# Reordering queues and the row chain of a fused ConvNeXt block and window graph block, and splitting its MLP step over halves and quarters of TensorE's array

## The chip, the cores and the metric

The kernel runs on one core of a Trainium2 chip. The metric is device time in microseconds (us) of one execution; three executions of the kernel before are the base. Lower is better.

## What is computed

The input `x` is 32 images of 24 channels, 56 by 56 pixels, in float32. Two blocks follow each other:

```python
# block 1 (ConvNeXt)
h = depthwise_conv_7x7(x) + conv_b
h = (h - mean_c(h)) * rsqrt(var_c(h) + 1e-5) * ln_g + ln_b     # over the 24 channels of a pixel
h = gelu(h @ w1 + b1)                                          # 24 -> 96
x1 = (h @ w2 + b2) * layer_scale + x                           # 96 -> 24
# block 2 (window graph)
y = (fc1(x1)) * s1 + t1                                        # 1x1 convolution
nodes = windows of 8 x 8 pixels of y                           # 64 nodes of 24 channels
idx = the 9 nearest nodes of each node, by distance of the normalised channel vectors
h = max over the 9 of gelu(([x_i, x_j - x_i] @ ew.T + eb) * es + et)   # 48 channels
out = fc2(h) * s2 + t2 + x1                                    # 48 -> 24
```

## The kernel before, in words

The program writes its own instruction streams for five engines (TensorE, VectorE, ScalarE, GpSimd and the DMA queue on SyncE), tied by semaphores. There is no scheduler: the order in each stream is the order in the code, and every engine works its stream in order. It has three stages.

**Convolution** (to about 200 us). Lines 861 to 876 on TensorE; the change does not touch it.

**MLP stage** (about 203 to 553 us), 56 steps `m` (`NSTEP`). A step takes four groups of 24 channels (32 partitions each, 24 of them used) by `L` = 448 pixels. Its parts on TensorE are functions: `centre` (L888, subtract the channel mean by a matmul, into bank 0), `variance` (L897, four matmuls with the squares of 112 pixels each as weights and 4 columns), `turn_std` (L904, four transposes of the spread reciprocal deviations, into bank 1), `expand` (L914, 24 to 96 channels: three matmuls of 128 by 128 by 448) and `contract` (L920, back to 24, four matmuls of 128 by 64 by 448 in column halves). `mlp_slot` (L930) orders them: contract of step m-1, centre of m+3, expand of m, turn of m+1, variance of m+3. VectorE's own `mlp_slot` (L712) does `residual(m-1)`, `spread_std(m+2)`, `normalise(m+1)`, `add_eps(m+3)`. GpSimd does one power per step (`inv_std`, L347), ScalarE one square, one copy and three gelus. `turn_std(m+1)` may overwrite bank 1 only after `normalise(m)` has read it (`at_least(pe, hn_d, m)`). SyncE loads `ht` (convolution output, `load_h`), `xt` (the input, `load_x`) and stores `x1_d` (`store_x1`) per pair of steps, four DMAs each.

**Graph stage** (about 581 to 2187 us). 28 iterations `i` (`NI`, strips of 8 image rows), each of 7 windows `wx`; one window is a "slot", 196 in all. In a slot `pe_slot` (L1068) finds distances for the window three ahead (`dist`), ranks for the one two ahead (`transpose`, `ranks`, `project`), splits projections into three bfloat16 parts (`subtract`), and gathers the neighbours by one-hot matmuls (`gather`, 3 of 12 matmuls each). VectorE (`dve_slot`, L802) reduces what was gathered (6 `reduce`, L783), builds eight one-hot masks (`make_onehot`, L770), takes the top 8 (L756) and marks them (L762). GpSimd's `pool_slot` (L389) adds the query term (`add_q`, L369).

Once per iteration, between the slots, stand the parts of the "row chain" for the next iteration: `fc1` in slots 5 and 6, `make_y` on ScalarE (L467), `norm` (L962, slot 0), the power on GpSimd (`inv_norm`, L361), `spread_norm` on VectorE (L747), `turn_norm` (L968, slots 1 and 2), `take_norm` on ScalarE, `scale_y` on GpSimd (L377, slot 2), `square_xa`, `halfsq` (L977, slot 3), `take_xb` (L488), four `spread_xa` copies on ScalarE (L494, slots 2 and 3: the four 32-partition blocks of `xa` go to a block-diagonal tile `xam`), six `node_terms` (L1004, placed by the table `QS_AT`) and `fc2` of the iteration before (L995, slots 4 and 5). `dist` waits for `xb_done` and `xam_done`. `node_terms` reads `y2`, which SyncE copies from `yb` (`load_y2`, L281, 12 DMAs), queued behind `store_iter`, `load_res` and `load_iter`.

The loops over pairs of iterations turn back at slot 0 of an even iteration on TensorE, and at slot 0 of an odd one on VectorE, ScalarE and GpSimd.

## Time and profile before

| | us |
|---|---|
| median of 3 runs | 2190.81 |
| lowest and highest | 2185.35, 2200.28 |
| the profiled execution, its own time | 2189.12 |
| its span, first to last instruction | 2187.2 |

Busy over the span: TensorE matmul 1919.6 us (88%), its weight loads 899.0 (41%, beside the matmuls), VectorE 1521.0 (70%), ScalarE 1113.3 (51%), GpSimd 643.8 (29%). The mean granted TensorE clock is 0.94 of full. The table shows what engines did, not what they cost: an idle engine costs nothing unless the chain that sets the end runs through it. Ends of matmuls are modelled, so distances between starts say more than durations; these are used below.

### The profile page before, as it was taken

The page shows a single profiled execution, that of the slowest core. Times are in us where ns is not written, and L with a number is a line of the kernel's source. Part 1 is how long each engine was busy: PE and PEld are TensorE (multiplying, and loading weights), DVE is VectorE, ACT ScalarE, POOL GpSimd, SP SyncE. Part 2 cuts the span into 40 slices and gives each one's busy share as a digit, 9 for nine tenths or more (in the row PEclk, how much of TensorE's full clock was granted, in tenths as well). Part 3 has the DMA queues.
Part 4 walks back from the last instruction along what each step waited for, and adds up shares of the span by engine and source line. Part 5 has one row for each costly group of instructions (what it writes and reads, how often), then busy time and mean ns, then how long its engine had stood idle before and what let it go on. Part 6 is the DMA issues. An engine that isn't in the chain of part 4 may idle for free.

```text
span 2187.2 us, 49786 instructions
## 1 busy us (share of the span) xinstructions
PE 1919.6 (88%) x16042; PEld 899.0 (41%) x16042; DVE 1521.0 (70%) x5840; ACT 1113.3 (51%) x2630; POOL 643.8 (29%) x407
## 2 busy tenths in 40 slices
PE   6998999999788898898888888888888888889886
PEld 2444555555333343343433333434343433434332
DVE  4222222222398889788888888888888888888897
ACT  0012444444465556565555555555555555656563
POOL 3002444444122322222222232222222222223232
PEclk9997999999799989899999999999999899989999
DMA  7872333333201111110111111111111111111010
GB/s 142 148 147 68 83 85 83 85 81 80 57 14 33 33 34 29 29 27 21 29 33 34 33 33 33 34 33 33 33 33 33 34 33 31 28 25 28 23 38 14
DMA packets 161305, 105.54 MB, mean 48 GB/s; under 512 B 120640, under 2 KB 158272, under 8 KB 160960
## 3 DMA queue, kind: packets, MB, share of 16 engines
q1 hardware_dynamic: 161088, 102.63, 20.5%
q8 instruction: 138, 2.26, 0.4%
q14 instruction: 79, 0.65, 0.1%
HBM read 54.40 MB, written 28.90 MB: 38 GB/s over the span
## 4 chain that ended last, share of the span: by engine, by line
PE 45%; issue 25%; ACT 12%; DVE 9%; POOL 6%; SPq 1%; DMA 1%; POOLq 0%; DVEq 0%; ACTq 0%
PE bank L867 7%; PE bank L1063 6%; PE bank L918 6%; PE bank L995 5%; ACT xam L494 4%; DVE red L783 4%; PE bank L926 4%; PE bank L892 3%; POOL hq L369 3%; POOL rn L361 2%; PE bank L1034 2%; ACT pb L510 2%; PE bank L1018 2%; PE bank L901 2%; DVE onehot L770 2%
## 5 line engine op out<-in xcount | busy, mean ns | idle before, releaser
L783 DVE TENSOR_REDUCE red<-bank 128x64 f32<-128x512 f32 x1176 | 751.6, 679 | 221.1 <-PE bank L1063 202.7
L510 ACT CAST pb<-bank 64x192 bf16<-64x192 f32 x1176 | 367.6, 313 | 391.7 <-PE bank L1034 361.5
L1063 PE MATMUL bank<-onehot,pb 128*32 128x512 bf16 x7056 | 517.3, 401 | 4.6 <-DVE red L783 4.0
L369 POOL TENSOR_TENSOR hq<-red,arena 128x384 f32<-128x384 f32 x196 | 201.8, 1029 | 548.5 <-DVE red L783 537.8
L350 POOL TENSOR_TENSOR rs<-ve,mhalf 112x16 f32<-112x16 f32 x56 | 162.4, 2899 | 351.6 <-DVE ve L689 351.6
L770 DVE TENSOR_SCALAR onehot<-slot 128x256 bf16<-128x256 bf16 x1568 | 244.2, 227 | 0.0
L1004 PE MATMUL bank<-arena,wqs 128*128 128x448 f32 x336 | 174.9, 605 | 55.3 <-DMA arena<-yb 51.6
L1063 PEld LDWEIGHTS bank<-onehot,pb 128*32 128x32 bf16 x7056 | 137.3, 97 | 183.4 <-issue 84.6
L361 POOL TENSOR_TENSOR rn<-nv,mhalf 128x28 f32<-128x28 f32 x28 | 135.9, 4854 | 219.3 <-DVE nv L742 219.3
L867 PE MATMUL bank<-arena,toep 120*120 120x448 f32 x384 | 161.6, 582 | 21.4 <-DVE arena L621 21.4
L1034 PE MATMUL bank<-pb,nidentb 128*128 128x192 bf16 x784 | 139.0, 261 | 38.8 <-ACT pb L510 38.8
L762 DVE MATCH_REPLACE8 marked<-t,bank 128x64 bf16<-128x64 f32 x784 | 158.2, 211 | 0.0
L1012 PE MATMUL bank<-negb,identb 128*128 128x256 bf16 x196 | 56.7, 289 | 113.1 <-DVE marked L762 50.4
L1018 PE MATMUL bank<-xb,xam 128*64 128x64 f32 x3136 | 143.2, 238 | 0.0
L756 DVE MAX8 t<-bank 128x8 f32<-128x64 f32 x784 | 119.8, 211 | 32.4 <-PE bank L1018 32.4
L918 PE MATMUL bank<-hn,w1g 128*128 128x448 f32 x336 | 137.3, 545 | 0.0
L377 POOL TENSOR_TENSOR xa<-rnt,yb 128x512 f32<-128x512 f32 (+1 forms) x56 | 63.5, 1134 | 235.4 <-ACT rnt L483 235.4
L1018 PEld LDWEIGHTS bank<-xb,xam 128*64 128x64 f32 x3136 | 115.1, 146 | 30.0 <-issue 11.3
L442 ACT ACTIVATE sq<-bank 128x448 f32<-128x448 f32 x56 | 30.4, 543 | 189.3 <-PE bank L892 189.3
L995 PE MATMUL bank<-og,f 128*128 128x448 f32 x280 | 117.4, 551 | 4.7 <-DVE og L798 4.7
L386 POOL TENSOR_TENSOR x1o<-x1o,xt 128x448 f32<-128x448 f32 x56 | 63.9, 1142 | 184.3 <-DVE onehot L770 177.1
L867 PEld LDWEIGHTS bank<-arena,toep 120*120 120x120 f32 x384 | 70.7, 184 | 111.5 <-issue 90.1
(92 smaller groups left out, 2570.0 us busy)
## 6 DMA issues: line engine op xcount, KB each, us to landing
arena<-yb SPq DMA_DIRECT2D x336, 56.0 KB, 2.0
arena<-in_x SPq DMA_DIRECT2D x24, 392.0 KB
ht<-conv_d SPq DMA_DIRECT2D x112, 84.0 KB
xt<-in_x SPq DMA_DIRECT2D x112, 84.0 KB
x_d<-x1o SPq DMA_DIRECT2D x112, 84.0 KB
ht<-x_d SPq DMA_DIRECT2D x112, 84.0 KB
xt<-x_d SPq DMA_DIRECT2D x56, 168.0 KB, 3.2
out<-x1o SPq DMA_DIRECT2D x112, 84.0 KB, 2.0
```

The costliest lines, as they stand in the source:

```text
L361: nc.gpsimd.tensor_tensor(rn[:, :], nv[:, :], mhalf[:, :], ALU.pow).then_inc(s["rn_done"], 1)
L369: nc.gpsimd.tensor_tensor(hq[:, :, :, :], red[:, k, :, :, :], qs[:, b, :, wx, :].unsqueeze(1).broadcast_to([128, 2, T, NN]), ALU.add).then ...
L510: last = nc.scalar.copy(pb[64 * u:64 * u + 64, k, part, :, :, u, :], src[64 * u:64 * u + 64, :, :, :])
L770: last = nc.vector.tensor_scalar(onehot[:, k, :, t, :], slot[:, k, :, :], float(t + 1 - 99), None, ALU.is_equal)
L783: nc.vector.tensor_reduce(red[:, k, h, t, :], src, axis=mybir.AxisListType.X, op=op).then_inc(s["red_done"], 1)
L867: last = mm(bank[0:KC, 2 * b + ch, 0:CL].rearrange("p (b v) -> p b v", v=W2), toep[b][:, sh, :], xrow[b][:, ICH * ch:ICH * (ch + 1), 2 * s ...
L918: mm(bank[:, 3 + t, 0:L], w1g[:, t, :], hn[:, r % 2, :], start=True, stop=True).then_inc(mm1_d, 1)
L995: last = mm(bank[:, 6 + gp, 0:L], f2[:, 2 * gp + t, :], og[:, b, t, :, :, :].rearrange("p r w c -> p (r w c)"), start=t == 0, stop=t == 1 ...
L1004: mm(bank[:, 5, 0:L], wqs[:, e // T, e % T, :], y2[:, b, e % T, :, :].rearrange("p w i -> p (w i)"), start=True, stop=True).then_inc(s["qs ...
L1018: last = mm(bank[64 * h:64 * h + 64, 2, t * NN:(t + 1) * NN], xam[:, b, wx, u, 2 * gp + h, :], xb[:, b, wx, u, :], start=False, stop=True, ...
L1034: last = mm(bank[:, 3, 0:G * O].rearrange("p (g c o) -> p g c o", g=G, c=NCH), nidentb[:, :], pb[:, k, part, :, :, u, :], start=False, sto ...
L1063: last = mm(bank[32 * q:32 * q + 32, (k + t) % 2, :], pb[:, k, part, g, c, :, :].rearrange("p u o -> p (u o)"), onehot[:, k, g, :, :].rear ...
```

## The change

**MLP step, TensorE.** `expand` does tile t=1 as two column halves of 64, and tiles t=0 and t=2, whose weights are nonzero only in rows 0 to 63 and 64 to 127, as four quarters of 64 by 64, into banks 3 and 5. `contract` and ScalarE's `gelu` take t=1 first. `variance` works on column halves of 64 pixels (8 matmuls), `turn_std` on blocks of 128 (three, and one of 64). `mlp_slot` now has the order turn (m+1), centre (m+4), variance (m+3), contract (m-1), expand (m). The order on VectorE stays.

**SyncE.** `h` is loaded one pair further ahead; `x1_d` is laid out as its tile, so that `store_x1` and `load_iter` are one DMA each of all 128 partitions; `load_y2` is 8 DMAs, and stands ahead of `load_iter`, `store_iter` and `load_res`; `load_res` is 4 DMAs.

**Row chain.** `norm` comes ahead of `dist` in slot 0, `norms` ahead of the second reduce on VectorE; all of `turn_norm` and `take_norm` are in slot 1; two of the four `spread_xa` are on GpSimd (as multiplies straight from `rnt` and `yb`, after VectorE's one-hots of slots 2 and 3); `square_xa` moves behind the copy of `slot`; `node_terms` start in slot 0; `fc2` of the second half is dealt out over slots 4 and 5.

```diff
-LB = L // NBLK
+LB = 128
-        QS_AT = (((), ()), ((0,), (1,)), ((2,), (3,)), ((), ()), ((), (4,)), ((), ()), ((), (5,)))
+        QS_AT = (((), (0,)), ((1,), (2,)), ((3,), (4,)), ((), ()), ((), ()), ((), ()), ((), (5,)))
...
             def store_x1(i, b):
                 sp.wait_ge(x1_dn, 2 * (i + 1))
-                for g in range(G):
-                    sp.dma_start(x1_d[i, g, :, :].rearrange("(u c) l -> c u l", u=2),
-                                 x1o[32 * g:32 * g + C, 2 * b:2 * b + 2, :]).then_inc(x1_out[b], 16)
+                sp.dma_start(x1_d[i, :, :, :], x1o[:, 2 * b:2 * b + 2, :]).then_inc(x1_out[b], 16)
...
-                for t in range(T):
-                    for blk in range(4):
-                        g, u = (t, 3)[blk // 2], blk % 2
-                        sp.dma_start(y2[32 * blk:32 * blk + 32, b, t, :, :], yb[32 * g:32 * g + 32, b, u, :, :]
+                for u in range(2):
+                    for t in range(T):
+                        sp.dma_start(y2[32 * u:32 * u + 32, b, t, :, :], yb[32 * t:32 * t + 32, b, u, :, :]
                                      ).then_inc(y2_in[b], 16)
+                    sp.dma_start(y2[64 + 32 * u:96 + 32 * u, b, :, :, :].rearrange("c t w i -> c t (w i)"),
+                                 yb[96:128, b, u, :, :].rearrange("c w i -> c (w i)").unsqueeze(1).broadcast_to([32, T, L])
+                                 ).then_inc(y2_in[b], 16)
...
-            with sp.Fori(0, NI // 2 - 2) as j:
+            with sp.Fori(0, NI // 2 - 3) as j:
                 for b in range(2):
-                    load_iter(2 * j + (b + 3), 1 - b)
-                    load_y2(2 * j + (b + 2), b)
+                    load_y2(2 * j + (b + 3), 1 - b)
+                    load_iter(2 * j + (b + 5), 1 - b)
                     store_iter(2 * j + b, b)
                     load_res(2 * j + (b + 2), b)
...
+            def spread_xa(i, b, g):
+                pool.wait_ge(s["xa_done"], 2 * (i + 1))
+                at_least(pool, s["dist_mm"], WX * (i - 1))
+                nc.gpsimd.tensor_tensor(xam[32 * g:32 * g + 32, b, :, :, g, :], rnt[32 * g:32 * g + 32, :, :, :],
+                                        yb[32 * g:32 * g + 32, b, :, :, :].rearrange("p u w i -> p w u i"), ALU.mult
+                                        ).then_inc(s["xam_pool"], 1)
+                pool.wait_ge(s["xam_pool"], 2 * i + (g - 1))
...
+                if ahead1 and pre and wx in (2, 3):
+                    pool.wait_ge(s["onehot_done"], n + 2)
+                    if wx == 3:
+                        pool.wait_ge(s["addq_done"], n)
+                    spread_xa(i + 1, (b + 1) % 2, wx)
...
             def expand(m, r):
                 pe.wait_ge(hn_d, m + 1)
-                for t in range(3):
-                    at_least(pe, gelu_d, 3 * (m - 1) + (t + 1))
-                    mm(bank[:, 3 + t, 0:L], w1g[:, t, :], hn[:, r % 2, :], start=True, stop=True).then_inc(mm1_d, 1)
+                for c in range(2):
+                    last = mm(bank[64 * c:64 * c + 64, 4, 0:L], w1g[:, 1, 64 * c:64 * c + 64], hn[:, r % 2, :],
+                              start=True, stop=True)
+                last.then_inc(mm1_d, 1)
+                for k, t in ((0, 0), (64, 2)):
+                    for c in range(2):
+                        last = mm(bank[64 * c:64 * c + 64, 3 + t, 0:L], w1g[k:k + 64, t, 64 * c:64 * c + 64],
+                                  hn[k:k + 64, r % 2, :], start=True, stop=True)
+                last.then_inc(mm1_d, 2)
...
-                if pre and wx == 2:
-                    turn_norm(i + 1, (4,))
+                if pre and wx == 0:
+                    norm(i + 1)
...
                 if post and wx == 4:
                     fc2(i - 1, bn, 0)
+                if post and wx == 5:
+                    fc2(i - 1, bn, 1, (1,))
...
-                    turn_norm(i + 1, (0, 1, 2, 3))
+                    turn_norm(i + 1, range(WX))
                 if pre and wx == 3:
-                    halfsq(i + 1, bn, 1, 0)
+                    halfsq(i + 1, bn, 1, 1)
+                if post and wx == 4:
+                    fc2(i - 1, bn, 1, (0,))
                 if post and wx == 5:
-                    fc2(i - 1, bn, 1)
+                    fc2(i - 1, bn, 1, (2,))
```

The first place is one MLP step on TensorE. Before, as written by the loop (L926 contract, L892 centre, L918 expand, L909 turn, L901 variance):

```order
L926 MATMUL bank<-gl,w2s 64x448 x3
L925 REGISTER_ALU
L926 MATMUL bank<-gl,w2s 64x448
L889 ISA
L892 MATMUL bank<-ht,par 128x448
L72 REGISTER_ALU
L918 MATMUL bank<-hn,w1g 128x448 x3
L909 MATMUL bank<-par,rse 128x112 x4
L898 REGISTER_ALU
L901 MATMUL bank<-par,sq 112x4 x4
```

And the step of the change (L935 turn, L914 centre, L925 variance, L956 contract, L943 the halves of expand, L948 its quarters):

```order
L935 MATMUL bank<-par,rse 128x128 x3
L935 MATMUL bank<-par,rse 128x64
L72 REGISTER_ALU
L914 MATMUL bank<-ht,par 128x448
L925 MATMUL bank<-par,sq 64x4 x8
L955 ISA
L956 MATMUL bank<-gl,w2s 64x448 x2
L955 REGISTER_ALU
L956 MATMUL bank<-gl,w2s 64x448 x2
L943 MATMUL bank<-hn,w1g 64x448 x2
L948 MATMUL bank<-hn,w1g 64x448 x4
```

Contract and expand are now the last two parts of a step and follow each other; the turn of the next step comes right behind expand.

The second place is slot 5 of an iteration on TensorE, from its second round of gathers to the end. Before (L995 is `fc2`, L958 `fc1`, L1063 a gather, L1044 transposes, L1034 subtract, L1027 project):

```order
L1034 MATMUL bank<-pb,nidentb 128x192 x2
L1044 MATMUL bank<-unmark,marked 128x128 x2
L1034 MATMUL bank<-pb,nidentb 128x192 x2
L72 ISA
L1063 MATMUL bank<-onehot,pb 32x512 x12
L1052 MATMUL bank<-mts,prefb 128x256
L995 MATMUL bank<-og,f 128x448 x3
L956 ISA
L72 ISA
L958 MATMUL bank<-ht,par 128x448
L1027 MATMUL bank<-wp,yb 64x192 x2
```

And of the change (L1026 is `fc2`, L989 `fc1`):

```order
L1067 MATMUL bank<-pb,nidentb 128x192 x2
L1026 MATMUL bank<-og,f 128x448
L1077 MATMUL bank<-unmark,marked 128x128 x2
L1067 MATMUL bank<-pb,nidentb 128x192 x2
L72 ISA
L1096 MATMUL bank<-onehot,pb 32x512 x12
L1085 MATMUL bank<-mts,prefb 128x256
L1026 MATMUL bank<-og,f 128x448
L987 ISA
L72 ISA
L989 MATMUL bank<-ht,par 128x448
```

Of the three matmuls of `fc2` that stood together in slot 5, one is now in the middle of the slot, one at its old place, and one at the end of slot 4.

## Rows read from the trace of the kernel before

**Rows 1.** Windows (PE, PEld, DVE, ACT, POOL busy, PEclk, DMA share, GB/s): MLP stage; two iterations.

```profile
203.00:553.00 350.00, 346.99 (x1572) 182.62 (x1573) 102.08 (x223) 158.27 (x283) 164.64 (x58) 0.99 0.33 80
1499.00:1615.00 116.00, 101.99 (x1006) 46.77 (x1006) 96.94 (x397) 66.87 (x167) 32.58 (x25) 0.91 0.13 31
```

**Rows 2.** Timeline (start, us, engine, line, [idle before]): one MLP step on TensorE.

```profile
401.00 0.55 PE L909 MATMUL bank<-par,rse 112*128 112x112 f32 x4
...
401.38 0.86 PE L901 MATMUL bank<-par,sq 128*112 128x4 f32 x8
...
402.18 1.72 PE L926 MATMUL bank<-gl,w2s 128*64 128x448 f32 x8
...
403.83 1.21 PE L892 MATMUL bank<-ht,par 128*128 128x448 f32 x2
...
404.88 2.42 PE L918 MATMUL bank<-hn,w1g 128*128 128x448 f32 x6
...
407.13 0.55 PE L909 MATMUL bank<-par,rse 112*128 112x112 f32 x4
```

**Rows 3.** Timeline of the same step, VectorE and GpSimd.

```profile
401.68 0.62 DVE L702 TENSOR_TENSOR hn<-bank,hcs 128x448 f32<-128x448 f32 x1 [1.98 <-PE bank L909]
...
402.54 2.90 POOL L350 TENSOR_TENSOR rs<-ve,mhalf 112x16 f32<-112x16 f32 x1 [3.23 <-DVE ve L689]
...
403.95 0.68 DVE L709 SCALAR_TENSOR_TENSOR x1o<-bank,b2s,xt 128x448 f32<-128x448 f32 x1 [1.49 <-PE bank L926]
...
405.47 0.36 DVE L695 COPY rse<-rs 112x384 f32<-112x384 f32 x1 [0.84 <-POOL rs L350]
```

**Rows 4.** Waits of VectorE over the whole span: what, in total us, times, longest.

```profile
DVE red L783 <- PE bank L1063: 202.7, 147, 4.6
```

**Rows 5.** Timeline of slot 5 and the first reduce of slot 6 (even iteration).

```profile
1602.69 0.34 PE L1034 MATMUL bank<-pb,nidentb 128*128 128x192 bf16 x2 [0.62 <-ACT pb L510]
...
1603.84 2.42 PE L995 MATMUL bank<-og,f 128*128 128x448 f32 x6
...
1608.31 0.69 DVE L783 TENSOR_REDUCE red<-bank 128x64 f32<-128x512 f32 x1 [1.60 <-PE bank L1063]
```

**Rows 6.** Timeline from the end of slot 3 through slot 4.

```profile
1590.66 1.89 ACT L494 COPY xam<-xa 32x896 f32<-32x896 f32 x2
...
1593.34 0.28 PE L1012 MATMUL bank<-negb,identb 128*128 128x256 bf16 x1 [1.11 <-ACT xb L488]
...
1593.55 0.69 PE L1018 MATMUL bank<-xb,xam 128*64 128x64 f32 x16
...
1597.89 0.69 DVE L783 TENSOR_REDUCE red<-bank 128x64 f32<-128x512 f32 x1 [0.97 <-PE bank L1063]
```

**Rows 7.** Timeline, slots 6, 0 and 1 (odd iteration), and a window of slot 1.

```profile
1553.58 0.72 ACT L467 ACTIVATE yb<-bank,c,par 128x448 f32<-128x448 f32 x1
...
1560.47 7.77 SPq L281 DMA_DIRECT2D arena<-yb  x12
...
1569.77 1.86 PE L1004 MATMUL bank<-arena,wqs 128*128 128x448 f32 x2 [1.86 <-DMA arena<-yb]
1565.00:1576.00 11.00, 9.14 (x58) 4.04 (x59) 7.74 (x29) 2.57 (x8) 3.75 (x2) 0.53 0.15 37
```

**Rows 8.** Timeline of TensorE in slot 0, at its loop's turn (even iteration).

```profile
1500.93 0.39 PE L1012 MATMUL bank<-negb,identb 128*128 128x256 bf16 x1 [2.97 <-issue]
...
1504.00 3.04 PE L965 MATMUL bank<-par,sq 128*128 128x4 f32 x14
```

**Rows 9.** Timeline of VectorE and GpSimd, slot 4 (first row) and slot 2.

```profile
1535.36 1.17 DVE L770 TENSOR_SCALAR onehot<-slot 128x256 bf16<-128x256 bf16 x8
...
1578.86 1.96 DVE L770 TENSOR_SCALAR onehot<-slot 128x256 bf16<-128x256 bf16 x8
...
1578.68 1.11 POOL L369 TENSOR_TENSOR hq<-red,arena 128x384 f32<-128x384 f32 x1
1581.29 0.99 POOL L377 TENSOR_TENSOR xa<-rnt,yb 128x384 f32<-128x384 f32 x1 [1.50 <-ACT rnt L483]
```

More of the change, by code:

```diff
@@ L406, in _ @@
                 scale_y(0, 0, k)
+            for g in (2, 3):
+                spread_xa(0, 0, g)
             for n in range(3 * WX):
@@ L587, in _ @@
                 take_xb(0, 0, u)
-            for g in range(G):
+            for g in range(2):
                 spread_xa(0, 0, g)
@@ L822, in dve_slot @@
                         dve.wait_ge(s["t8_done"], G * (n + 4))
-                if pre and wx == 0:
-                    norms(i + 1)
                 if gather:
@@ L900, in variance @@
                 for k in range(NBLK):
-                    last = mm(bank[0:LB, 2, G * k:G * k + G], sq[:, LB * k:LB * k + LB], P("mean4"), start=True, stop=True)
+                    for half in range(2):
+                        a = min(LB * k + 64 * half, L - 64)
+                        last = mm(bank[64 * half:64 * half + 64, 2, G * k:G * k + G], sq[:, a:a + 64], P("mean4"),
+                                  start=True, stop=True)
                 last.then_inc(var_d, 1)
@@ L946, in _ @@
                 variance(m)
+            centre(3, 3, 0)
             turn_std(0, 0)
```

113 lines of the change are left out of this document (59 added, 54 removed).

## The prediction

> **What bounds the kernel now.** I read the busy shares by stage first, then the timeline of one MLP step, then VectorE's waits and the timeline of two graph iterations. Two stages matter for the change.
>
> In the MLP stage TensorE is busy 347.0 of 350 us for 56 steps, VectorE 102 us, ScalarE 158 us and GpSimd 165 us [rows 1]. TensorE is the bound: every ns taken from its step counts, until another chain becomes the longer one. One step lasts 407.13 - 401.00 = 6.13 us. From start to start its parts take: turn 0.38, variance 0.80, contract 1.65, centre 1.05, expand 2.25 [rows 2]. Expand is three matmuls, so one 448-column fp32 matmul takes 0.75. Contract is four half matmuls and takes 1.65, about two of these: two column halves already run beside each other here.
>
> The graph stage is 14 pairs of iterations of 116 us. In one pair VectorE is busy 96.9 and TensorE 102.0 [rows 1]. Neither is full: they hand work to each other. VectorE is the one to follow: its reduces, masks and rankings stand in every slot, and its idle time, 116.0 - 96.9 = 19.1 us of the pair, is time by which the slots are late. Over the span its largest wait by far is for gathers: 202.7 us [rows 4]. So I asked for each gap what TensorE was doing instead of the gather. Four kinds came out. In slot 5 the three matmuls of `fc2` (2.42 us) and a `fc1` stand ahead of the next gather, and VectorE waits 1.60 us [rows 5]. After slot 3 `dist` waits 1.11 us for `xb`, because ScalarE does two `spread_xa` (1.89 us) first, and VectorE then waits 0.97 us late in slot 4 [rows 6]. In slot 1 of an odd iteration TensorE waits 1.86 us for the `y2` copies, and a stretch at a granted clock of 0.53 follows in which VectorE is busy 7.74 of 11 us [rows 7]. In slot 0 of an even iteration TensorE is idle 2.97 us at its loop's turn, and seven `norm` matmuls then take 3.04 us [rows 8].
>
> **MLP step.** On TensorE, in units of rows 2. Turn: the same 448 columns, 0.39. Centre: 1.05. Variance: 8 column-half matmuls, 16 hardware passes. The nearest row is `dist`, 16 passes of 64 weight columns in 0.69 us with the tail [rows 6], some 0.45 to the next start; the old row is the other bound, 0.80. I take 0.5. Contract: 1.50, since it now follows work of the same column halves. Expand: one round for the two halves of t=1, 0.75, and one for the four quarters if all four run together, 0.75. TensorE alone would need 0.39 + 1.05 + 0.5 + 1.50 + 1.50 = 4.94. Changes of array shape come on top: contract's 1.65 against two times 0.75 shows 0.15 for a change in and out, and the new step has four or five such changes for two before; I add 0.25, 5.2 in all.
>
> The Trainium skill (TensorEngine Tiling (Array Packing), Key Properties) says that changing the tiling mode drains TensorE while changing only the tile does not; by that rule, too, the quarters pay at their two borders, and the 0.15 of the row is its price here, so the sum stays.
>
> But the new order makes VectorE's chain late. The turn of the next step needs `spread_std` and `normalise`, and both stand behind `residual`, which waits for contract, now followed only by expand. From contract's start the residual starts 403.95 - 402.18 = 1.77 us later; then come 0.68, 0.36 and 0.62 [rows 2, 3], and some 0.1 for the semaphore: 3.53. TensorE reaches the turn at 1.50 + 1.50 + 0.15 = 3.15. So the step is 3.53 plus turn 0.39, centre 1.05, variance 0.5 and a change of 0.1: 5.6 us (5.57), with TensorE idle 0.4 us ahead of each turn. It saves 6.13 - 5.6 = 0.53, times 56: 30 us. GpSimd's 2.90 us power [rows 3] starts after `add_eps`, at the end of VectorE's group, and has until the next group, over 3.5 us, so it is not late; ScalarE has 158/56 = 2.8 us of work in 5.6. Bounds: 5.2 (VectorE hidden), 52 us; 6.0 if the quarters run as two pairs one after the other (0.75 more on TensorE, 3.9 from contract's start), 7 us. I stay at 30, since all its durations are rows. Nothing in the trace shows row quarters.
>
> DMA: a share of 0.33 in this stage [rows 1] leaves room; fewer and longer transfers and earlier loads are worth nothing while no step waits for them.
>
> **Graph stage, per pair of iterations.** (a) `fc2` dealt out: in slot 5 one of three matmuls (0.81) goes to slot 4, where a `node_terms` leaves, and one goes to mid-slot, where TensorE waits 0.62 for ScalarE anyway [rows 5]. The gather comes 0.81 + 0.62 = 1.43 earlier, of a wait of 1.60. Twice: 2.8 us. (b) `spread_xa`: ScalarE does one copy of 0.94 less before `xb`, `dist` starts about 1 us earlier, and the 0.97 in slot 4 goes. Twice: 1.9. The 0.9 us at the end of slot 3 stay, since TensorE's four `halfsq` fill it. (c) `y2` in the odd iteration: y is done at 1554.30, but the issue of its 12 copies starts at 1560.47 and takes 7.77, 0.65 each [rows 7]. Now 8 follow at once: 5.2 us, and with the 1.5 from last issue to use, `y2` is there at about 1561.0, or 1562.5 if the two three-fold copies are slower. Its user stood at 1567.9 (1569.77 - 1.86) and now stands late in slot 0, by my estimate at 1561 to 1562. So the 1.86 wait goes, or up to 1.5 of it stays, one slot earlier. What it gives is mostly the slow clock behind it: VectorE's 3.3 idle us in the 11 us window [rows 7] at most (above, 11.0 - 7.74), nothing at least, if the remaining gaps still bring the lower level. I take 2.0. (d) `node_terms` 0 now stands in slot 0 of the even iteration, where TensorE is the bound and at half clock (3.04 us for norm) [rows 8]: a loss of 0.9 to 1.9, I take 1.0. Putting `norm` ahead of `dist` only changes the order within it. (e) GpSimd beside VectorE: a group of one-hot masks that takes 1.17 in slot 4 took 1.96 in slot 2 beside an add of GpSimd, so it is held; the second `scale_y` (0.99) came only 1.5 us after that add, when the masks were done [rows 9]. With both norms taken in slot 1 it follows the add at once, and can hold the masks up to 0.99 more: 2.0 a pair at most, I take 1.0. The two spreads on GpSimd start after the masks, beside reduces that read PSUM, and I price them at nothing; what they cost if that cover fails is the last rival.
>
> Sum: 2.8 + 1.9 + 2.0 - 1.0 - 1.0 = 4.7 a pair, 66 us over 14. What is late next is TensorE, 102 of 116 us. Ahead of the first slot the first `y2` stands open with nothing beside it: four issues fewer, 2.6 us.
>
> **Sum.** 30 + 66 + 3 = 99 us from the profiled execution's own 2189.1 (its span is 2187.2): 2090. That execution lies 1.7 us under the median, 2190.8, so I say 2092.
>
> **Rivals.**
> - *The clock stays up.* Without the `y2` wait the odd iteration keeps the full clock, (c) gives 3.3, and (d) and (e) cost nothing: 2.8 + 1.9 + 3.3 = 8.0 a pair, 112 us; with 33: 2044. For it: the 0.53 stretch begins right after TensorE's gaps. Against: the loop turns that make the other gaps stay.
> - *Gaps come up elsewhere.* Half of (a) and (b) returns in the next slot, (c) gives nothing, (d) costs its 1.0: 2.35 - 1.0 = 1.35 a pair, 19 us; with 33: 2137. For it: TensorE has only 14 us of slack in 116.
> - *The quarters do not run together.* 7 instead of 30: 2113. The change would then not do what it says. For it: no row shows row quarters; against: column halves do run together.
> - *Slower: GpSimd holds VectorE.* A spread of 896 columns at the rate of 0.99 us for 384 [rows 9] is 2.3 us; four a pair are 9.2, with (e) at its full 2.0 it is 11.2 against gains of 2.8 + 1.9 + 2.0 - 1.0 = 5.7: 5.5 a pair lost, 77 us, less 33: 2233. It decides from 8 us a pair on. For it: rows 9 show masks held for nearly the whole overlap. Against: the code lets a spread start only after the masks, and what follows there is mostly reduces with one input, in PSUM.
>
> The Trainium skill (GPSIMD Engine Reference, the table of its head, "SBUF interfaces") says that GpSimd contends with VectorE instructions in a 2-port mode or with two SBUF inputs. By it the masks, `og` and `mx` suffer and the reduces do not; the trace agrees as far as the held mask of rows 9 goes, so this rule speaks for the loss in (e), and against the whole of the last rival.
>
> **How the numbers follow.** Forecast 0.50, clock up 0.12, gaps elsewhere 0.20, quarters apart 0.12, slower 0.06. A measurement of this kernel tells about 1% (22 us) from no change. Faster by over 1%: 0.92; within: 0.03; slower by over 1%: 0.05. The range reaches to the first rival and past the second: 2042 to 2152.
>
> **What would show it.** MLP: turns 5.6 us apart, TensorE idle 0.3 to 0.5 ahead of each, released by `normalise`; the starts of expand's matmuls fall on four points 0.375 apart, and on six if the quarters run apart. If turns are 5.2 apart the chain on VectorE was hidden. Graph: no 1.6 wait ahead of slot 6's first reduce, no 1.1 wait for `xb`, the `y2` wait gone from slot 1; a pair of about 111 us. A one-hot group of 3 us in slot 2, or reduces longer than 0.7, would show GpSimd in the way. Wrong would be a pair above 114.5 or below 107, or an MLP step above 5.9.

## The result, and the profile after the change

| | before | after |
|---|---|---|
| median of 4 runs | 2191.1 us (2185.35 to 2200.28) | 2059.12 us (2056.85 to 2063.14) |
| profiled execution, own time | 2189.1 us | 2063.14 us |
| its span | 2187.2 us | 2061.3 us |

The ratio is 0.9396, 95% interval 0.9359 to 0.9432: 6.0% faster. The forecast was 2092 us, 99 us less. Measured are 132 us between the medians, and 126 us between the two profiled executions, whose stages are compared here.

The two spans divided at marks that both traces have (the first `centre`, the last `residual`, the first and the last group of one-hot masks on VectorE):

| stage | before | after | difference | forecast |
|---|---|---|---|---|
| convolution, to the first `centre` | 192.7 | 180.9 | -11.8 | 0 |
| MLP, first `centre` to last `residual` | 356.3 | 335.5 | -20.7 | -30 |
| last `residual` to first masks | 37.65 | 37.84 | +0.2 | -2.6 |
| graph, first to last masks | 1577.1 | 1483.1 | -94 | -66 |

A pair of graph iterations takes 107.7 us on average over twelve pairs (before 115.7 by the same marks). A window of the MLP stage after the change, which answers to [rows 1] (columns as there), then the same twelve pairs in the kernel before and in the changed kernel:

```profile
203.00:509.00 306.00, 301.58 (x2231) 117.01 (x2231) 84.11 (x213) 147.68 (x266) 150.77 (x52) 1.00 0.35 97
...
685.41:2074.14 1388.73, 1206.70 (x12076) 554.03 (x12073) 1163.99 (x4753) 804.28 (x1992) 396.47 (x288) 0.93 0.13 32
...
655.46:1948.07 1292.61, 1202.83 (x12076) 547.31 (x12072) 1136.39 (x4753) 756.11 (x1944) 529.84 (x336) 0.92 0.14 36
```

Per pair, TensorE's and VectorE's idle time both fell (15.2 to 7.5 us and 18.7 to 13.0). VectorE's busy time fell too (97.0 to 94.7), though its instructions are the same 4753. GpSimd has 11 us more, and the granted clock is nearly as before (0.93 and 0.92).

Waits of VectorE and of TensorE over the span, which answer to [rows 4] and to the `y2` wait of [rows 7] (what, total us, times, longest):

```profile
DVE red L805 <- PE bank L1096: 107.7, 95, 2.5
DVE nv L764 <- PE bank L996: 38.4, 12, 3.5
```

```profile
PE bank L996 <- issue: 39.8, 11, 3.8
...
PE bank L1036 <- DMA arena<-yb: 5.0, 1, 5.0
PE bank L935 <- DVE hn L724: 3.2, 13, 0.8
```

The wait for gathers fell from 202.7 to 107.7. A wait for `norm` (L996) is new among the large ones. The wait for `y2` is left once, before the first slot.

One MLP step on TensorE and VectorE, to be read against [rows 2, 3] (L935 turn, L914 centre, L925 variance, L956 contract, L943 halves, L948 quarters; L731 residual, L717 `spread_std`, L724 normalise):

```profile
402.23 0.75 PE L935 MATMUL bank<-par,rse 128*128 128x128 f32 x4
402.91 1.21 PE L914 MATMUL bank<-ht,par 128*128 128x448 f32 x2
404.05 0.64 PE L925 MATMUL bank<-par,sq 128*64 128x4 f32 x16
404.54 1.70 PE L956 MATMUL bank<-gl,w2s 128*64 128x448 f32 x8
406.07 0.92 PE L943 MATMUL bank<-hn,w1g 128*64 128x448 f32 x4
406.92 0.98 PE L948 MATMUL bank<-hn,w1g 64*64 64x448 f32 x8
407.92 0.72 PE L935 MATMUL bank<-par,rse 128*128 128x128 f32 x4
```

```profile
406.29 0.68 DVE L731 SCALAR_TENSOR_TENSOR x1o<-bank,b2s,xt 128x448 f32<-128x448 f32 x1 [4.04 <-PE bank L956]
406.89 0.35 DVE L717 COPY rse<-rs 128x384 f32<-128x384 f32 x1
407.16 0.62 DVE L724 TENSOR_TENSOR hn<-bank,hcs 128x448 f32<-128x448 f32 x1
```

The step is 407.92 - 402.23 = 5.69 us. From contract's start the chain over VectorE takes 407.92 - 404.54 = 3.38. TensorE itself is through at 1.53 + 0.85 + 0.92 = 3.30 (the 0.92 is taken from m2_residual_last below, where nothing is waited for). The two are nearly level.

Slot 0 of an even iteration, TensorE and then VectorE, to be read against [rows 8]:

```profile
1413.85 3.14 PE L996 MATMUL bank<-par,sq 128*128 128x4 f32 x14 [3.75 <-issue]
...
1422.86 1.70 PE L1036 MATMUL bank<-arena,wqs 128*128 128x448 f32 x2
```

```profile
1417.03 0.19 DVE L764 TENSOR_SCALAR nv<-bank 128x28 f32<-128x28 f32 x1 [3.44 <-PE bank L996]
1419.74 1.29 DVE L805 TENSOR_REDUCE red<-bank 128x64 f32<-128x512 f32 x2 [2.52 <-PE bank L1096]
...
1422.80 1.29 DVE L805 TENSOR_REDUCE red<-bank 128x64 f32<-128x512 f32 x2 [1.24 <-PE bank L1096]
...
1426.77 1.29 DVE L805 TENSOR_REDUCE red<-bank 128x64 f32<-128x512 f32 x2 [1.89 <-PE bank L1096]
```

Here VectorE waits 9.1 us in one slot (3.44 + 2.52 + 1.24 + 1.89), where a whole pair has 13.0 on average. One `node_terms` (L1036) takes 1.70, and 0.92 elsewhere: the granted clock from 1422.8 to 1424.6 us is 0.50, the lower of the two levels (1.2 instead of 2.4 GHz).

Slot 2, VectorE and GpSimd, which answers to [rows 9], and VectorE's reduces that answer to the last ones of [rows 5, 6]:

```profile
1435.18 1.18 DVE L792 TENSOR_SCALAR onehot<-slot 128x256 bf16<-128x256 bf16 x8
...
1452.64 1.29 DVE L805 TENSOR_REDUCE red<-bank 128x64 f32<-128x512 f32 x2 [0.56 <-PE bank L1096]
...
1461.55 1.29 DVE L805 TENSOR_REDUCE red<-bank 128x64 f32<-128x512 f32 x2
```

```profile
1434.87 2.61 POOL L378 TENSOR_TENSOR hq<-red,arena 128x384 f32<-128x384 f32 x1
```

The masks beside GpSimd's add took 1.96 before; now they take 1.18, and the add takes 2.61 instead of 1.11. The wait of 1.60 us is gone (the last row has none), and 0.97 became 0.56.

### The profile page after: what moved, and what is told of

It reads as the page before. It is cut to its first block, busy times and chain, and to the rows that moved or that the text cites. A ratio compares the mean times of both kernels' runs of the same rounds, so it can differ in the third digit from the quotient of the medians.

```text
span 2061.3 us, 51002 instructions
## 1 busy us (share of the span) xinstructions
PE 1897.3 (92%) x16826; PEld 836.8 (41%) x16826; DVE 1470.3 (71%) x5840; ACT 1056.6 (51%) x2574; POOL 798.1 (39%) x463
## 4 chain that ended last, share of the span: by engine, by line
PE 71%; DVE 13%; ACT 9%; issue 5%; DMA 1%; SPq 1%; DVEq 0%; POOL 0%; ACTq 0%; POOLq 0%
PE bank L1096 15%; PE bank L889 8%; DVE red L805 6%; PE bank L1051 5%; PE bank L1026 5%; PE bank L1036 4%; PE bank L956 4%; PE bank L1067 4%; PE bank L914 3%; PE bank L996 3%; PE bank L1060 3%; DVE onehot L792 2%; PE bank L1013 2%; PE bank L989 2%; PE bank L935 2%
## 5 line engine op out<-in xcount | busy, mean ns | idle before, releaser
L805 DVE TENSOR_REDUCE red<-bank 128x64 f32<-128x512 f32 x1176 | 757.4, 690 | 133.0 <-PE bank L1096 107.7
L378 POOL TENSOR_TENSOR hq<-red,arena 128x384 f32<-128x384 f32 x196 | 236.3, 1205 | 381.8 <-DVE red L805 376.5
L359 POOL TENSOR_TENSOR rs<-ve,mhalf 128x16 f32<-128x16 f32 x56 | 162.4, 2900 | 316.1 <-DVE ve L711 316.1
L792 DVE TENSOR_SCALAR onehot<-slot 128x256 bf16<-128x256 bf16 x1568 | 232.9, 227 | 0.0
L731 DVE SCALAR_TENSOR_TENSOR x1o<-bank,b2s,xt 128x448 f32<-128x448 f32 x56 | 38.3, 684 | 227.1 <-PE bank L956 227.1
L1036 PE MATMUL bank<-arena,wqs 128*128 128x448 f32 x336 | 180.5, 622 | 8.7 <-DMA arena<-yb 5.0
L475 ACT ACTIVATE gl<-bank,b1s 128x448 f32<-128x448 f32 x168 | 100.3, 631 | 91.4 <-PE bank L943 74.6
L386 POOL TENSOR_TENSOR xa<-rnt,yb 128x512 f32<-128x512 f32 (+1 forms) x56 | 63.2, 1130 | 200.6 <-ACT rnt L509 200.6
L394 POOL TENSOR_TENSOR xam<-rnt,yb 32x896 f32<-32x896 f32 x56 | 118.1, 2109 | 44.9 <-DVE onehot L792 40.7
L1026 PE MATMUL bank<-og,f 128*128 128x448 f32 x280 | 127.8, 557 | 5.5 <-DVE og L820 5.5
L1060 PE MATMUL bank<-wp,yb 128*64 128x192 f32 x784 | 114.3, 372 | 0.3 <-ACT pb L536 0.3
```

The source lines that it names most:

```text
L359: nc.gpsimd.tensor_tensor(rs[:, :], ve[:, :], mhalf[0:LB, 0:NBLK * G], ALU.pow).then_inc(pow_d, 1)
L378: nc.gpsimd.tensor_tensor(hq[:, :, :, :], red[:, k, :, :, :], qs[:, b, :, wx, :].unsqueeze(1).broadcast_to([128, 2, T, NN]), ALU.add).then ...
L792: last = nc.vector.tensor_scalar(onehot[:, k, :, t, :], slot[:, k, :, :], float(t + 1 - 99), None, ALU.is_equal)
L805: nc.vector.tensor_reduce(red[:, k, h, t, :], src, axis=mybir.AxisListType.X, op=op).then_inc(s["red_done"], 1)
L1026: last = mm(bank[:, 6 + gp, 0:L], f2[:, 2 * gp + t, :], og[:, b, t, :, :, :].rearrange("p r w c -> p (r w c)"), start=t == 0, stop=t == 1 ...
L1036: mm(bank[:, 5, 0:L], wqs[:, e // T, e % T, :], y2[:, b, e % T, :, :].rearrange("p w i -> p (w i)"), start=True, stop=True).then_inc(s["qs ...
```

## The experiments

All but the runs of the kernel before are edits of the changed kernel. Ratios are against the kernel before on the same chip. "MLP" and "graph" are the stages of the table above.

| run | median us (runs) | ratio, 95% | MLP step | MLP | graph |
|---|---|---|---|---|---|
| changed kernel | 2059.12 (4) | 0.9396 [0.9359, 0.9432] | 5.69 | 335.5 | 1483.1 |
| m1_halves | 2072.27 (2) | 0.9465 [0.9441, 0.9488] | 6.20 | 362.0 | 1465.8 |
| m2_residual_last | 2049.05 (4) | 0.9363 [0.9333, 0.9394] | 5.61 | 330.4 | 1469.4 |
| m3_old_order | 2050.15 (2) | 0.9364 [0.9339, 0.9389] | 5.80 | 335.0 | 1469.4 |
| g1_fc2_whole | 2087.92 (2) | 0.9532 [0.9486, 0.9579] | 5.69 | 334.8 | 1502.8 |
| g2_spread_act | 2102.76 (2) | 0.96 [0.9572, 0.9628] | 5.69 | 335.6 | 1523.0 |
| g3_node_late | 2046.45 (2) | 0.9343 [0.9304, 0.9381] | 5.69 | 334.8 | 1465.1 |
| g4_norm_back | 2053.0 (2) | 0.9373 [0.9345, 0.94] | 5.69 | 334.6 | 1473.4 |
| g5_y2_late | 2091.7 (2) | 0.9557 [0.9538, 0.9577] | 5.69 | 335.8 | 1510.3 |
| c1_combined | 2041.06 (4) | 0.932 [0.9262, 0.9378] | 5.32 | 317.1 | 1489.7 |
| c2_node_late_whole_turn | 2033.8 (4) | 0.9308 [0.9272, 0.9344] | 5.32 | 317.6 | 1458.0 |
| before_again | 2180.13 (1) | | 6.13 | 355.0 | 1567.7 |
| b1_memset_wait | 2178.87 (3) | 0.9962 [0.994, 0.9983] | 6.13 | 356.2 | 1577.3 |

The changed kernel, m1, m2 and m3 have the same graph stage: 1483.1, 1465.8, 1469.4, 1469.4, mean 1471.9. They spread over 17 us, the changed kernel's own profile being the longest. So a graph stage is compared with their mean, 1472, and differences under 10 us are not read. The kernel before, three times (with b1): 1577.1, 1567.7, 1577.3, mean 1574. The graph stage gained 102 by these means.

**m1_halves.** The quarters again as column halves over all 128 rows; the rest as changed.

```diff
-                for k, t in ((0, 0), (64, 2)):
+                for t in (0, 2):
...
-                        last = mm(bank[64 * c:64 * c + 64, 3 + t, 0:L], w1g[k:k + 64, t, 64 * c:64 * c + 64],
-                                  hn[k:k + 64, r % 2, :], start=True, stop=True)
+                        last = mm(bank[64 * c:64 * c + 64, 3 + t, 0:L], w1g[:, t, 64 * c:64 * c + 64],
+                                  hn[:, r % 2, :], start=True, stop=True)
```

> The changed kernel, but expand does t=0 and t=2 as column halves over all 128 rows instead of quarters. Theory A (the four quarters run together, 0.75 us; the step is set by VectorE's chain residual, spread_std, normalise at 3.53 us from contract's start): TensorE needs 0.75 us more and reaches the turn 3.9 us after contract's start, so the step goes from 5.69 to about 6.0 us, 17 us in all. Rival B (the quarters run as two pairs one after the other): nothing changes, 5.7 us a step.

The two tiles take 1.60 to the next turn instead of 0.92, and the step is 6.20:

```profile
405.92 1.67 PE L948 MATMUL bank<-hn,w1g 128*64 128x448 f32 x8
407.52 0.75 PE L935 MATMUL bank<-par,rse 128*128 128x128 f32 x4
```

So the four quarters do run together. The step grew by more than the 0.3 expected, since TensorE and the chain over VectorE were already nearly level. The quarters are worth 0.51 us a step and 26.5 us in the stage. Without them the new order is 5.7 us longer than the old stage (362.0 against 356.3): in this order all of the stage's gain is the quarters'.

**m2_residual_last.** `residual` behind `spread_std`, `normalise` and `add_eps` on VectorE.

```diff
-                if not first:
-                    residual(m - 1, (r - 1) % NBUF, old)
...
                 if now + 3 < end:
                     add_eps(m + 3)
+                if not first:
+                    residual(m - 1, (r - 1) % NBUF, old)
```

> The changed kernel, but VectorE does spread_std, normalise and add_eps ahead of residual. Theory A (TensorE idles 0.4 to 0.7 us ahead of each turn because residual, which waits for contract, stands first on VectorE): the idle goes, the step falls from 5.69 to 5.2 us, 27 us in all, about 2032 us. Rival B (the gap ahead of the turn is the change of the array's shape, not VectorE): the step stays at 5.7 us and the time at 2059.

The chain over VectorE is out of the way, and TensorE's own work is left:

```profile
401.82 1.70 PE L956 MATMUL bank<-gl,w2s 128*64 128x448 f32 x8
403.35 0.92 PE L943 MATMUL bank<-hn,w1g 128*64 128x448 f32 x4
404.20 0.98 PE L948 MATMUL bank<-hn,w1g 64*64 64x448 f32 x8
405.12 0.75 PE L935 MATMUL bank<-par,rse 128*128 128x128 f32 x4
405.80 1.21 PE L914 MATMUL bank<-ht,par 128*128 128x448 f32 x2
406.94 0.64 PE L925 MATMUL bank<-par,sq 128*64 128x4 f32 x16
407.43 1.70 PE L956 MATMUL bank<-gl,w2s 128*64 128x448 f32 x8
```

Contract 1.53, halves 0.85, quarters 0.92, turn 0.68, centre 1.14, variance 0.49: 5.61, where the forecast, and the expectation of this run, had 5.2. Only 5.1 us of the stage (335.5 to 330.4) were the chain's.

**m3_old_order.** TensorE's order as before the change (contract, centre three ahead, expand, turn, variance), with ScalarE's squares three ahead; quarters and halves stay.

```diff
+                if not first:
+                    contract(m - 1, r - 1)
+                if now + 3 < end:
+                    centre(m + 3, r + 3, j + (r + 3) // NBUF)
+                expand(m, r)
                 if now + 1 < end:
                     turn_std(m + 1, r + 1)
-                if now + 4 < end:
-                    centre(m + 4, r + 4, j + (r + 4) // NBUF)
```

> The changed kernel with TensorE's old step order (contract m-1, centre m+3, expand m, turn m+1, variance m+3), quarters, column halves and t=1 first kept. Theory A (the gain of the stage comes from the quarters and the halves of variance, the order adds a wait): contract can wait some 0.1 to 0.3 us for the gelus but no turn waits for residual: 5.3 to 5.5 us a step, under the 5.69 of the changed kernel. Rival B (the order is what made room): contract waits for the gelus by 0.5 us or more, the step is 5.8 us or longer.

The step is 0.11 longer, but the first `residual` comes at 200.3 us instead of 207.1, since less has to be filled, and the stage is the same (335.0). The new order gives back at the start what it saves in the steps. The step has the 5.8 us of the run's rival B, but not with its wait of 0.5 us for the gelus: over the whole run TensorE's matmuls wait 0.4 us for them, and its weight loads 11.2. Theory A's 5.3 to 5.5 was too low, as the forecast's 5.2 was.

**g1_fc2_whole.** The second half of `fc2` as three matmuls late in slot 5, as before.

```diff
-                if post and wx == 5:
-                    fc2(i - 1, bn, 1, (1,))
...
-                if post and wx == 4:
-                    fc2(i - 1, bn, 1, (0,))
                 if post and wx == 5:
-                    fc2(i - 1, bn, 1, (2,))
+                    fc2(i - 1, bn, 1)
```

> The changed kernel with the second half of fc2 back in one place, late in slot 5. Theory A (dealing it out removed VectorE's wait of 1.6 us ahead of slot 6's first reduce): the wait comes back, up to 1.4 us an iteration, 2.8 a pair: a pair of 109.4 us against 106.6, 39 us in all. Rival B (slot 6 has slack by now, the gain came from elsewhere): a pair stays within 1 us.

The wait at the end of slot 5 is back, in every iteration, and the slot takes 8.42 instead of 6.70:

```profile
1473.91 1.29 DVE L805 TENSOR_REDUCE red<-bank 128x64 f32<-128x512 f32 x2 [1.81 <-PE bank L1096]
```

1502.8 - 1472 = 31 us, 2.2 a pair, as theory A had it. The forecast's term (a) was 2.8. (In 8 of 24 slots 2 of this run the masks are held, as in the kernel before, so the price is not of `fc2` alone.)

**g2_spread_act.** All four `spread_xa` on ScalarE, two each in slots 2 and 3.

```diff
-                    spread_xa(i + 1, (b + 1) % 2, wx - 2)
+                    for g in (2 * wx - 4, 2 * wx - 3):
+                        spread_xa(i + 1, (b + 1) % 2, g)
```

(and GpSimd's two are taken out.)

> The changed kernel with all four spread_xa on ScalarE, none on GpSimd. Theory A (two copies fewer ahead of xb let dist of slot 4 start 1 us earlier): dist waits for xb again and a pair grows by up to 1.9 us, 27 us in all. Rival B (the spreads on GpSimd hold VectorE as much as they free): no change, or faster.

Waits of TensorE, where the changed kernel has 18.7 in this row, and ScalarE in the slot:

```profile
PE bank L1038 <- ACT xb L507: 50.0, 27, 1.9
```

```profile
1477.62 1.89 ACT L513 COPY xam<-xa 32x896 f32<-32x896 f32 x2
1479.53 0.53 ACT L507 COPY xb<-bank 128x448 f32<-128x448 f32 x1
```

The interval from slot 3 to 4 is 7.86 in most iterations instead of 6.86, and that from 4 to 5 between 8.58 and 10.2 instead of 7.40. In sum 51 us, 3.6 a pair; the forecast's term (b) was 1.9, for it followed the 0.97 us of slot 4 alone. This is the price in the changed kernel, where slot 4 also holds more of `fc2`: the kernel before, with the same four copies on ScalarE, took 7.81 from slot 4 to 5.

**g3_node_late.** `node_terms` at their old slots.

```diff
-        QS_AT = (((), (0,)), ((1,), (2,)), ((3,), (4,)), ((), ()), ((), ()), ((), ()), ((), (5,)))
+        QS_AT = (((), ()), ((0,), (1,)), ((2,), (3,)), ((), ()), ((), (4,)), ((), ()), ((), (5,)))
```

> The changed kernel with node_terms at their old slots (1, 1, 2, 2, 4, 6), y2 still copied early. Theory A (what made slot 1 of the odd iteration slow was the wait for y2 and the slow clock behind it, and the copies alone cure it; node_terms 0 in slot 0 of the even iteration only costs, where VectorE now idles 9.1 us): a pair is 1 to 2 us shorter. Rival B (the moved node_terms fill TensorE's gaps, or make room for fc2 in slot 4): a pair is 1 us longer or more.

The clock stays at its upper level far more (0.97 against 0.92 over the same twelve pairs), slot 0 to 1 of an even iteration takes 10.5 to 11.2 (once 12.6) instead of 13.2 to 16.2 (once 11.9), and `norm` there takes 1.82 instead of 3.14. Waits of VectorE, which had 38.4 in this row:

```profile
DVE nv L764 <- PE bank L996: 14.1, 12, 2.8
```

```profile
655.27:1929.90 1274.63, 1149.30 (x12080) 528.81 (x12072) 1169.25 (x4753) 753.47 (x1944) 512.80 (x336) 0.97 0.13 36
```

But slots 2 to 3 and 4 to 5 take 8.15 each instead of 6.88 and 7.40. In slot 2 the reason is GpSimd: the masks, 1.18 in the changed kernel, take 2.79 here, in every iteration, over the add and the second `scale_y` (L386):

```profile
1425.32 2.79 DVE L792 TENSOR_SCALAR onehot<-slot 128x256 bf16<-128x256 bf16 x8
...
1425.14 1.11 POOL L378 TENSOR_TENSOR hq<-red,arena 128x384 f32<-128x384 f32 x1
1426.21 1.00 POOL L386 TENSOR_TENSOR xa<-rnt,yb 128x384 f32<-128x384 f32 x1
```

Slot 4 holds a `node_terms` again. Gain and loss come to 7 us, less than the scatter; c2, with the same edit, has 14 less. So the early `node_terms` have cost time, if anything, as term (d) said. The edit moves five of the six, so what each costs is not shown. The price goes with a lower clock in slot 0, and what the held masks add here, 2 x (2.79 - 1.18) = 3.2 us of VectorE a pair, hides part of it.

**g4_norm_back.** `norm` and `norms` at their old places (TensorE: behind the first gathers of the slot; VectorE: behind `top8`).

```diff
-                if pre and wx == 0:
-                    norm(i + 1)
...
+                if pre and wx == 0:
+                    norm(i + 1)
                 if pre and wx == 3:
                     halfsq(i + 1, bn, 0, 1)
```

> The changed kernel with norm and VectorE's norms back at their old places in slot 0, behind dist, the gathers and the top 8. Theory A (VectorE stands at norms for 3.4 us with reduces behind it, and that is most of what slot 0 of the even iteration lost, 13.1 to 16.1 us): a pair is 2 to 3 us shorter, unless the power on GpSimd comes late again and holds rne and mx (up to 2 us back). Rival B (slot 0 is bound by TensorE's work at half clock in whatever order): within 1 us, or longer by the held rne.

1473.4: no difference, as the run's rival B had it. VectorE's wait for `norm` falls to 13.6 us, its longest wait for gathers grows from 2.5 to 4.7, and TensorE's wait for `y2` grows from 5.0 to 22.5, since `node_terms` 0 comes sooner. In 14 of 24 slots 2 the masks are held, which the changed kernel has in none. Where `norm` stands is not what makes slot 0 long.

**g5_y2_late.** As g3, and `load_y2` as 12 copies behind `store_iter`, `load_res` and `load_iter`.

```diff
-                    load_y2(2 * j + (b + 3), 1 - b)
-                    load_iter(2 * j + (b + 5), 1 - b)
                     store_iter(2 * j + b, b)
                     load_res(2 * j + (b + 2), b)
+                    load_iter(2 * j + (b + 5), 1 - b)
+                    load_y2(2 * j + (b + 3), 1 - b)
```

> Like g3_node_late, and with y2 again in 12 copies, behind store_iter, load_res and load_iter. Theory A (the early copies are what cured slot 1 of the odd iteration, 12.9 to 7.2 us in g3_node_late): the wait of some 2 us and the slow clock behind it come back, slot 1 of odd iterations takes 11 to 13 us, a pair 110 us or more against 106.2, 55 us in all. Rival B (TensorE has so much less to wait for elsewhere that the clock stays up and y2 costs its bare wait or nothing): a pair grows by under 2 us.

Against g3 the graph stage is 45 us longer (1510.3 - 1465.1), 3.2 a pair, as theory A had it (a pair takes 110.1 us; slot 1 of odd iterations 9.5 and not 11 to 13). Waits of TensorE (g3 has 3.2 in this row), and one of them:

```profile
PE bank L1034 <- DMA arena<-yb: 30.0, 16, 5.3
```

```profile
1502.49 1.01 PE L1034 MATMUL bank<-arena,wqs 128*128 128x448 f32 x2 [2.39 <-DMA arena<-yb]
1506.61 1.29 PE L1034 MATMUL bank<-arena,wqs 128*128 128x448 f32 x2
```

27 us are the wait itself. The rest, 18, goes with a slower clock behind it: the second row takes 1.29, which is 0.92 in g3, and the mean granted clock of slot 1 of odd iterations is 0.96 instead of 1.00, of slot 0 there 0.85 instead of 0.94.

**before_again.** The kernel before once more, for the scatter of its stages.

> The kernel before, for a second profile: in the first the convolution stage, whose code is the same in both kernels, took 192.7 us to the first centre, and 180.9 in the changed kernel. If this is scatter of the DMA traffic at the start, it comes out anywhere between 178 and 196 here; if it is of the kernel, at 192 to 193.

The stages are those of the first profile within 10 us, and the long first stage (193.1) is there again.

**b1_memset_wait.** The kernel before, with GpSimd's later memsets held back until the convolution's copies are done.

```diff
             nc.gpsimd.memset(mhalf[:, :], -0.5).then_inc(mhalf_set, 1)
+            pool.wait_ge(conv_dup, C)
             nc.gpsimd.memset(rse[:, :, :, :, :], 0.0)
```

> The kernel before, with GpSimd's memsets of the tiles of the later stages moved behind the last copy of VectorE in the convolution (one wait). Theory A (in both profiles of the kernel before VectorE's first copy stands from about 9 to 21.3 us while GpSimd clears those tiles; in the changed kernel it gets in between two memsets, so 11 us of the measured gain are an accident of that order): the first copy takes 1.2 us, TensorE starts at 10.4 instead of 21.4 us, the first centre comes at 182 us, and the kernel before gains 11 us, to about 2179. Rival B (the copy waits for its data, the memsets are beside it): nothing changes.

The first stage falls from 192.7 to 180.9, as in the changed kernel, and no other stage moves beyond its scatter; the whole is 0.4% faster. The start of the convolution in the kernel before, in the changed one, and in this one:

```profile
8.78 14.73 DVE L621 COPY arena<-arena 56x1952 f32<-56x1952 f32 x3 [5.88 <-DMA toep<-in_zfilt]
...
12.28 6.08 POOL L342 MEMSET xam<- 128x7168 f32 x1
...
21.39 3.34 PE L867 MATMUL bank<-arena,toep 120*120 120x448 f32 x4 [21.39 <-DVE arena L621]
```

```profile
8.88 1.43 DVE L643 COPY arena<-arena 56x1952 f32<-56x1952 f32 x1 [5.98 <-DMA toep<-in_zfilt]
...
9.23 2.62 POOL L349 MEMSET ht<- 128x1792 f32 x1
...
10.37 14.04 PE L889 MATMUL bank<-arena,toep 120*120 120x448 f32 x30 [10.37 <-DVE arena L643]
```

```profile
8.55 1.17 DVE L622 COPY arena<-arena 56x1952 f32<-56x1952 f32 x1 [5.66 <-DMA toep<-in_zfilt]
...
9.78 14.59 PE L868 MATMUL bank<-arena,toep 120*120 120x448 f32 x30 [9.78 <-DVE arena L622]
```

VectorE's copy of 1.2 us is held in the kernel before until the memsets are through at about 20 us, and TensorE starts at 21.39. In the changed kernel the copy gets in, and a memset is stretched (2.62 instead of 1.59).

**c1_combined, c2_node_late_whole_turn.** Both have m2's edit and turn whole blocks of 128 columns, so that the turn's four transposes have one shape. c1 has b1's wait too and `node_terms` 4 in slot 6; c2 has g3's slots.

```diff
-                    size = min(LB, L - LB * k)
-                    last = nc.tensor.transpose(bank[:, 1, LB * k:LB * k + size],
-                                               rse[0:size, r % 2, k, :, :].rearrange("p g c -> p (g c)"),
-                                               P("ident")[0:size, 0:size])
+                    last = nc.tensor.transpose(bank[:, 1, LB * k:LB * k + LB],
+                                               rse[:, r % 2, k, :, :].rearrange("p g c -> p (g c)"), P("ident"))
```

> The changed kernel with four edits: residual last on VectorE; turn_std in four whole blocks of 128 rows, so that no block of 64 rows changes the array's shape twice; node_terms at slots 1, 1, 2, 2, 6, 6; the memsets behind the convolution's copies. Theory A (a change of shape costs 0.1 to 0.15 us each time; slot 4 was late by node_terms 4 and slot 0 by node_terms 0): the MLP step falls from 5.61 (m2_residual_last) to 5.35 us, 15 us in all; a pair falls from 106.2 (g3_node_late) to 105, 17 us; about 2015 us. Rival B (the 64-row block costs its columns only, and node_terms 4 makes slot 6 late instead): 5.6 us a step, 106.2 a pair, about 2045 us.

> The changed kernel with three edits: residual last on VectorE, turn_std in four whole blocks of 128 rows, node_terms at their old slots as in g3_node_late. Theory A (the stages add up: 5.32 us a step as in c1_combined, a pair of 106.2 us as in g3_node_late, the steady half of whose gain is that the clock stays up): 2046 less 56 times 0.36, about 2026 us. Rival B (the clock's level in the graph stage is up to chance rather than to the kernel, so g3_node_late was a lucky one): pairs of 107 to 108 us, 2040 to 2050 us, as c1_combined.

The turn and what follows in c2, against 0.68 and 1.14 in m2:

```profile
404.90 0.66 PE L934 MATMUL bank<-par,rse 128*128 128x128 f32 x4
405.39 1.11 PE L914 MATMUL bank<-ht,par 128*128 128x448 f32 x2
406.43 0.64 PE L925 MATMUL bank<-par,sq 128*64 128x4 f32 x16
```

Turn 0.49, centre 1.04: 0.29 us a step, though 64 more columns are turned. That the last block of the turn (64 by 64) is a change of shape in and out had not been counted. c2 is the fastest median here, 2033.8 us, 1.2% under the changed kernel's (0.9% by the ratios). c1's median lies 7 us above it, within their scatter (c1 2031.09 to 2055.8, c2 2021.06 to 2045.86). c1's graph stage is longer, 1489.7, with pairs between 105.6 and 112.5. The MLP step came out as both expected (5.35 and 5.32). The pairs did so in c2's profile (105.6 us on average, 106.2 expected), but that is c2's fastest run, and the median lies 8 us above the 2026 expected. They did not in c1's (108.0 instead of 105). In both the masks of slot 2 are held in all 24 slots of the twelve pairs.

## Why the prediction was right, and where its steps were not

The forecast held (2059.12 in a range of 2042 to 2152). Its main mechanisms, (a) to (c) and the quarters, are shown by the runs. But several sizes are off, two of them in opposite directions (the MLP stage gained 9 us less than forecast, the graph stage 28 more), 11.8 us come from a place that no step had, and the time is nearer to the first rival. The prediction's own sign of being wrong, a pair below 107 us, was nearly met: the profile has 107.7, and the three runs with the same graph stage have 106.3 to 106.6. Its sign "TensorE idle 0.3 to 0.5 ahead of each turn" did fail.

The graph stage by intervals, from the start of the masks of a slot to those of the next, mean of twelve pairs, in us a pair (g3 is g3_node_late):

| interval | before | after | g3 |
|---|---|---|---|
| slot 0, even iteration | 11.97 | 14.75 | 10.86 |
| slot 0, odd | 6.62 | 8.99 | 7.02 |
| slot 1, even | 8.46 | 6.94 | 7.19 |
| slot 1, odd | 12.47 | 6.94 | 7.18 |
| slot 2, both | 14.36 | 13.74 | 16.30 |
| slots 3 and 4, both | 31.07 | 28.52 | 30.12 |
| slot 5, both | 16.42 | 13.42 | 13.30 |
| slot 6, both | 14.35 | 14.43 | 14.25 |
| sum | 115.7 | 107.7 | 106.2 |

- **MLP step: 5.69, forecast 5.57.** That the two lie so close is partly luck. The chain was as said: `residual` 1.75 after contract's start (forecast 1.77), 3.38 to the turn (3.53). The step that failed is "TensorE alone 5.2". It is 5.61 in m2: what comes on top of the bare parts is 5.61 - 4.94 = 0.67 and not 0.25. Of it 0.29 go with the small block in the turn (c2), 0.10 stand between halves and quarters (0.85 to the next start, where m1 without that border has 0.75), 0.17 between quarters and turn (0.92 against 0.75); the last 0.1 is not assigned. So TensorE loses 0.08 on average and not 0.4 ahead of a turn, and it waits there for `normalise` in only 13 steps. The stage gave 20.7 and not 30: 56 x 0.44 = 24.6, less some 5 us of filling (the first `residual` comes 26.1 us after the first `centre`, before 21.1), which no term had. The Trainium skill (TensorEngine Tiling (Array Packing), Key Properties) says that a change of tiling mode drains TensorE. The runs agree in that each border measured costs time: 0.10, 0.17, and 0.29 us for the small block in the turn.
- **(a) 2.8 a pair, measured 2.2 (g1), and 3.0 in slot 5 from before to after.** Right.
- **(b) 1.9, measured 3.6 (g2), and 2.6 in slots 3 and 4 from before to after.** The mechanism was right, the size too small. With all copies on ScalarE both intervals behind them grow, by 1.0 and by 1.2 to 2.8 (g2). The term took one wait from one slot.
- **(c) 2.0, measured 3.2.** The wait went, with a higher clock behind it, as said: slot 1 of odd iterations fell from 12.47 to 6.94 us, and its mean granted clock rose from 0.72 to 1.00. But in the changed kernel slot 0 of odd iterations has 0.64, where it had 0.93, and takes 2.4 us more; in g3 it keeps 0.94. The wait is dearer than the 1.86 us of one row, for it came 22 times with 51.6 us in all. A total over the span would have been the row to read. The 8 issues took 5.1 to 7.9 us, 6.6 in the median, not the 5.2 forecast, and still came in time.
- **(d) -1.0.** Sign right as far as the scatter lets one say (7 us in g3, 14 in c2, over 14 pairs: 0.5 to 1.0). The near agreement hides larger parts: the two slots 0 grew by 5.2 us a pair from before to after and are 5.9 shorter in g3, which pays 2.6 in slot 2, for the held masks, and 1.5 in slot 4. The term looked at the even iteration alone.
- **(e) -1.0: wrong in sign in the changed kernel, right in sign where `node_terms` stand late.** In the changed kernel the masks are held in none of the 24 slots 2 of the twelve pairs (before in 19), and GpSimd's add takes 2.55 to 2.62 in their place. Over the span the masks take 232.9 us instead of 244.2, 0.8 a pair; another 0.9 a pair of VectorE's fall is the copy of the spread norms (`rne`, 14.2 instead of 26.7). In g3 and c2 the masks are held in all 24, for 2.79 us, the "one-hot group of 3 us" that the prediction named as a sign: 0.83 more than the 1.96 of before, of 0.99 forecast. These kernels are still not slower, since their slot 0 is shorter. What decides who is held is not shown. By the records the add starts first each time: 0.17 to 0.22 us ahead of the masks where it holds them (before, g3), 0.24 to 0.31 ahead where it is held itself (the changed kernel). The Trainium skill (GPSIMD Engine Reference, Specifications, "SBUF interfaces") names the contention, and the trace agrees that it is there.
- **The first `y2`: 2.6, measured 0.** The stretch from the last `residual` to the first masks is the same in the two profiles, 37.65 and 37.84, and scatters over the other runs with the early copies from 36.1 to 38.1; TensorE still waits 5.0 us for that `y2`.
- **Not forecast: 11.8 in the convolution,** which the change does not mean to touch. b1 shows it to be GpSimd's memsets holding VectorE's first copy.
- **Rivals.** The quarters run together (m1). The slower rival fell: with two spreads of 2.11 us an iteration on GpSimd the reduces stay at 0.64 each, and taking the spreads from GpSimd costs 51 us (g2). "The clock stays up" (2044) came nearer than the forecast, with the right size for a pair (8.0, measured 8.0), but by the wrong reason: the mean granted clock of the pairs is 0.92, as low as before (0.93), and (b), (c) and (e) came out better than forecast.

The single runs' prices add to 31 + 51 + 45 - 7 = 120 of a measured 102 us. They overlap: each edit puts a different work last, and some of them also change whether the masks of slot 2 are held (none of 24 in the changed kernel, 8 in g1, 5 in g2, 24 in g3, 14 in g4, 21 in g5).

Open: why in the kernel before the memsets come ahead of VectorE's copy and in the changed one not. Their starts differ by 0.1 us, and the memset of `rse` covers 128 partitions instead of 112; neither was tried alone. Open too is what scatters c1 and c2 over 25 us, and what c2 would take if its masks were not held (3.2 us a pair of VectorE).

## What to carry to other kernels

Price a wait by its total over the span and by all slots that it makes late, not by one row. When work is packed into pieces of the array, count each border between shapes (here 0.1 to 0.3 us), and pad an odd last block when that makes one shape of a run. When an edit moves work on one engine, look again at every place where GpSimd and VectorE work at the same time: here 0.1 us in their starts went with masks of 1.18 or 2.79 us, and the time hardly showed it. Work that nothing waits for (memsets) belongs behind the first work of the critical path.
